# Third and fourth batch: second GroupNorm two batches in front, first convolution's rows in the tail before, convolutions in earlier slots

## The reference

```
x = x + mix(groupnorm(x))       # s = relu(xn.T xn)**2 over the 1024 pixels; y = (W0 x + b0) s
x = x + deform(groupnorm(x))    # offset = conv3x3(conv3x3(x, w1, b1), w2, b2): 72 channels
                                # val = bilinear samples of x at 9 taps x 4 groups, moved by offset
                                # relu(einsum('ogck,bgckhw->bohw', wd, val))
```

## Time and profile before

| | us |
|---|---|
| median of 3 runs (460.49 to 461.5) | 460.77 |
| the profiled execution's own time | 459.05 |
| its span, first to last instruction | 457.0 |
| PE busy, share of the span | 405.2, 89% |
| DVE busy | 339.5, 74% |
| ACT busy | 215.6, 47% |
| POOL busy | 90.0, 20% |
| mean granted TensorE clock (1 is 2.4 GHz) | 0.970 |

### The profile page before, as it was taken

How to read it: one execution, slowest core, us unless ns; L and a number is a source line. 1 busy time by engine, 2 the same in 40 slices (tenths; PEclk the granted TensorE clock), 3 DMA queues, 4 the chain that set the end, 5 groups by cost and what they waited for, 6 DMA issues and landing times.

```text
span 457.0 us, 9689 instructions
## 1 busy us (share of the span) xinstructions
PE 405.2 (89%) x3887; PEld 291.9 (64%) x3887; DVE 339.5 (74%) x586; ACT 215.6 (47%) x392; POOL 90.0 (20%) x99
## 2 busy tenths in 40 slices
PE   6698989979998789799999798989869898979996
PEld 6455557646665565678666575768556566857875
DVE  5995776829999999388854999376979945779901
ACT  3343254345555365441655446331845643257661
POOL 5444470001774100000546100000010000000000
PEclk9899999999999899999999899989979997999999
DMA  7200002250011124332001313442213243303330
GB/s 252 77 0 0 0 2 75 84 141 1 2 47 46 47 67 146 85 90 91 12 13 36 92 54 94 124 126 81 59 47 100 90 122 98 104 23 107 96 105 24
DMA packets 46157, 32.71 MB, mean 72 GB/s; under 512 B 3264, under 2 KB 43488, under 8 KB 46112
## 3 DMA queue, kind: packets, MB, share of 16 engines
q1 hardware_dynamic: 46048, 31.95, 23.5%
q10 hardware_dynamic: 64, 0.13, 0.1%
HBM read 25.24 MB, written 10.37 MB: 78 GB/s over the span
## 4 chain that ended last, share of the span: by engine, by line
PE 46%; DVE 32%; DMA 6%; SPq 5%; issue 4%; ACT 4%; POOL 1%; DVEq 0%; ACTq 0%; POOLq 0%
PE psB L788 10%; PE psB L555 9%; PE psT L739 7%; DVE wpix L1507 7%; PE psV L762 5%; DVE combo L1294 4%; PE psA L646 4%; DMA h_scr<-h_ring 3%; SPq L320 3%; DVE combo_p L1298 2%; DVE tent L1488 2%; PE psA L555 2%; DVE tent L1482 2%; PE psB L813 2%; PE psA L813 2%
## 5 line engine op out<-in xcount | busy, mean ns | idle before, releaser
L1021 ACT ACTIVATE wcell<-psT 128x512 f32<-128x512 f32 (+1 forms) x160 | 83.9, 552 | 70.2 <-PE psT L739 68.9
L1507 DVE TENSOR_TENSOR wpix<-tent 128x512 f32<-128x512 f32 (+1 forms) x160 | 99.7, 675 | 14.4 <-PE psT L739 13.3
L739 PE MATMUL psT<-ident,wpix 128*128 128x128 f32 x576 | 89.1, 288 | 12.4 <-ACT wcell L1021 12.0
L739 PEld LDWEIGHTS psT<-ident,wpix 128*128 128x128 f32 x576 | 68.8, 148 | 37.2 <-issue 29.5
L493 POOL TENSOR_TENSOR sim<-rel 128x512 f32<-128x512 f32 x48 | 61.4, 1299 | 69.0 <-ACT rel L978 69.0
L1045 ACT ACTIVATE val<-psV 128x576 f32<-128x576 f32 x64 | 44.0, 688 | 30.7 <-PE psV L762 30.2
L788 PE MATMUL psB<-val,wd_sb 128*128 128x256 f32 x216 | 51.2, 392 | 0.0
L762 PE MATMUL psV<-wcell,hwin 64*32 64x144 f32 x2048 | 47.2, 294 | 3.9 <-ACT val L1045 3.5
L646 PE MATMUL psA<-sim,scratch 128*128 128x512 f32 x96 | 45.6, 597 | 0.6 <-POOL sim L493 0.6
L788 PEld LDWEIGHTS psB<-val,wd_sb 128*128 128x128 f32 x216 | 40.7, 193 | 8.3 <-issue 2.9
L555 PE MATMUL psB<-g_p 128*128 128x512 f32 x144 | 40.9, 419 | 0.0
(11 more groups left out here) (193 smaller groups left out, 453.6 us busy)
## 6 DMA issues: line engine op xcount, KB each, us to landing
hwin<-h_scr SPq DMA_DIRECT2D x128, 128.0 KB, 2.9
h_scr<-h_ring SPq DMA_DIRECT2D x8, 576.0 KB
h_ring<-sim SPq DMA_DIRECT2D x4, 512.0 KB
x_all<-x SPq DMA_DIRECT2D x1, 1536.0 KB, 10.0
out<-yout SPq DMA_DIRECT2D x12, 128.0 KB, 1.8
off_scr<-sim SPq DMA_DIRECT2D x4, 288.0 KB
combo<-sim SPq DMA_DIRECT2D x32, 32.0 KB
val<-w SPq DMA_DIRECT2D x1, 576.0 KB, 6.1
```

The lines of the kernel that those rows point to most:

```text
L739: last = pe.transpose(bank[:, at:at + P], wpix[:, t % 2, k, 2 * h:2 * h + 2, :].rearrange("p g q -> p (g q)"), ident[:, :])
L1021: act.activation(wcell[:, t % 2, taps[0]:taps[-1] + 1, :, :].rearrange("q k h p -> q (k h p)"), bank[:, 0:len(taps) * G // 2 * P], ACT.Cop ...
L1507: dve.tensor_tensor(w, ty, tx, ALU.mult).then_inc(s["weights_done"], 1)
```

## The change

Batches 2 and 3 get new tables. Their second GroupNorm is done in slots 57 to 60 of the loop two batches before. The rows of their first convolution (four combines, highs and lows) are done in the tail of that loop, in steps -8 to -1 that stand between the tail's instructions. In the loop before theirs the convolutions stand at slots 28 and 41 in place of 36 and 49 for batch 2 (`IN_FRONT`), and spread from slot 4 to 17 and from 26 to 40 for batch 3 (`SPREAD_OUT`); wrapping, turning of offsets and the next weights move up with them. Batch 1's table is unchanged. `lay_image` is issued behind the windows of tile 7 in every loop. The last batch's extremes and the flag move into the fourth loop. Because `combo` is now taken at that time, batch 3's diagonal moves to `sim`.

```diff
+        ROWS_AHEAD = ((-8, -8, -5, -3), (-6, -4, -2, -1), (-8, -7, -4, -2))      # combine, low, high
+        SPREAD_OUT = dict(combine=[ROWS_AHEAD[0], (18, 18, 21, 23)], low=[ROWS_AHEAD[1], (20, 21, 23, 24)],
+                          high=[ROWS_AHEAD[2], (19, 20, 22, 24)], conv=[(4, 7, 8, 13, 16, 17), (26, 29, 31, 34, 35, 40)],
+                          copy=[9, 32], sums=[16, 36], rows=[18, 41], mean=None, dev=None, var=None, norm=None, flat=2,
+                          image=22, wrap=42, shift=None, turn={56: (0, 1), 58: (2, 3)}, extremes=None)
+        AHEAD = dict(mean=57, dev=57, var=59, norm=60)
+        IN_FRONT = dict(in_a_row((29, 35), (30, 36), (28, 41)), mean=None, ..., flat=2, image=27,
+                        wrap=47, shift=None, turn={58: (0, 1), 60: (2, 3)}, extremes=66)
+        LEAD_WEIGHTS, FIRST_WEIGHTS, AHEAD_WEIGHTS, LAST_WEIGHTS, LEAD_EXTREMES = 60, 67, 62, 60, 12
+        LAST_EXTREMES, LAST_FARTHEST, LAST_FLAG = 24, 42, 46
...
 # SyncE
+                    image, shifts = ((5, 7), (4, 6), (5, 6))[min(b, 2)]
-                    if t == IMAGE_TILE + 1 and b + 1 < B:
-                        lay_image(b + 1)
...
                 else:
+                    lay_image(b + 1)
                     for t in range(2):
                         windows(b + 1, t)
...
 # ScalarE, behind the slots
+                rows_ahead(-8, -7)
                 relu_out(b, 0)
+                rows_ahead(-7, -6)
                 take_samples(b, ROWT - 1, 0)
+                rows_ahead(-6, -3)
                 take_samples(b, ROWT - 1, 1)
+                rows_ahead(-3, 0)
                 for m in range(1, 4):
                     relu_out(b, m)
...
 # VectorE, behind the slots
+                rows_ahead(-8)
                 add_out(b, 0)
-                if nxt is not None:
-                    for i in range(len(TAPS)):
-                        weights(nxt, 1, i)
+                for i in range(len(TAPS)):
+                    weights(nxt, 1, i)
+                    rows_ahead(i - 6)
+                rows_ahead(-1)
                 for m in range(1, 4):
                     add_out(b, m)
```

More of the change, by code:

```diff
@@ L881, in batch_steps @@
                                 prepare(prep, what)
-                        if nxt is not None and n == STEADY_IMAGE:
+                        if FIRST_AHEAD <= b + 2 < B:
+                            for col, step in enumerate(("mean", "var")):
+                                if n == AHEAD[step]:
+                                    group_mean(b + 2, col)
+                        if nxt is not None and n == front(nxt)["image"]:
                             turn_image(nxt)
                         if nxt is not None:
-                            conv_front(nxt, n, STEADY, prep)
+                            conv_front(nxt, n, front(nxt), prep)
                 if b == LAST:
@@ L994, in conv_front @@
                     m = 2 * b + which
[L995 to L999, removed]
+                    for v in range(V):
+                        if n == at["high"][which][v]:
+                            act.wait_ge(s["combo_done"], V * m + v + 1)
+                            act.activation(combo_p[:, 0, v], combo[:, v % 2], ACT.Copy).then_inc(s["combo_hi"], 1)
+                    if n == at["copy"][which]:
                         bias, width = ((b1_col, C), (b2_col, NOFF))[which]
@@ L1431, in conv_front @@
                 for which in range(2):
[L1432 to L1436, removed]
+                    for v in range(V):
+                        if n == at["combine"][which][v]:
+                            combine_rows(b, which, v)
+                    for v in range(V):
+                        if n == at["low"][which][v]:
+                            split_rows(b, which, v)
+                    if n == at["sums"][which]:
                         middle_sums(b, which)
-                    if n == at["conv"][which] + 5:
+                    if n == at["rows"][which]:
                         output_rows(b, which)
@@ L1620, in batch_steps @@
                         if nxt is not None:
[L1621 to L1622 removed]
+                            conv_front(nxt, n, front(nxt))
+                        if b == LAST and n == LAST_EXTREMES:
+                            find_extremes(LAST)
+                            find_farthest()
+                        if b == LAST and n == LAST_FLAG:
+                            set_flag()
+                        if FIRST_AHEAD <= b + 2 < B:
+                            if n == AHEAD["dev"]:
+                                spread(b + 2)
+                            if n == AHEAD["norm"]:
+                                normalise_x1(b + 2)
+                        for tile, slots in (W_EVEN if nxt == LAST else W_FRONT if nxt == FIRST_AHEAD else W_AT).items():
                             for i in range(len(TAPS)):
```

96 lines of the change are left out of this document (62 added, 34 removed).

## The result

The changed kernel takes 478.38 us (median of four runs, 476.56 to 480.77), the kernel before 461.05 beside it (460.49 to 461.50): a ratio of 1.0383, 95% interval 1.0345 to 1.0421. It is 17.3 us slower, on the side that was forecast, and 6.4 us above the top of the range. The profiled execution took 480.77 us with a span of 479.0 at a mean granted clock of 0.939 (0.970 before). It is the longest of the four, and the profiled execution of before is shorter than its own median, so the two spans lie 22.0 us apart.

The account below looks back on a forecast made before the run. PE was taken as close to the bound, with its idle time and slow clock in loops 1 and 2 to win. Terms +11.0, +3.0, -11.0 and +1.2 made +4.2 on a median of 460.77: 465.0 us, range 462 to 472.

Parts of the forecast that it names:

- Loop 0's tail: Tail of loop 0: ACT's in-order wait for new rows stops PE; +11.0 us, between +9.3 and +12.8.
- the second stop: Loop 0's tail: PE idle 3 us ahead of piece 2, waiting for the copy of tile 7's second half.
- Loop 1: Loop 1: convolutions and offsets come earlier, but DVE's late chain and clock lengthen it; +3 us, from 0 to +6.
- The chain itself: Loop 1 behind the offsets: DVE's work until 304.0, then 8.2 us to the copy of tile 7's second half.
- the clock's 1.8: Loop 1: three stops of 3 to 4.5 us cost up to 3.5 us of clock; 1.8 taken.
- PE stands about 4.5 us there: Loop 1: PE's wait while the shifted offsets land, where it stood 1.85 us before the change.
- Loop 2: Loop 2: with rows ready and no mixing on DVE, it falls from 84.7 to 73.8 us; -11, from -15 to -6.
- the walk: Loop 2's step-by-step estimate: second convolution's end at 36 us, offsets at 47, loop's end at 71.3 before clock loss.
- Loop 3: Loop 3 and strips: late stores delay DVE's weights, extremes and flag join its list; +1.2 us, 0 to +2.5.
- The flag's own wait is covered by 16 slots.: Loop 3: the flag is set early enough that PE does not wait for it; no cost booked.
- 1 to 2 us in tile 5: Loop 3: PE's wait for weights because DVE starts some 4 us late and has extremes to do.
- much slower: Rival: tail stops keep PE at 1.2 GHz through pieces 2 and 3, every term at its upper end; +15, 476 us; chance 0.12.

Follow-up runs that it names:

- e1: Changed kernel with one edit: in ACT's tail, piece 0 and both halves of tile 7 stand ahead of the rows' highs; 467.73 us, ratio 1.0177.
- e2: Changed kernel with one edit: SP issues a tail's first two stores ahead of the next batch's windows; 475.55 us, ratio 1.0346.
- e3: Changed kernel with one number changed: DVE sets the flag in slot 36 rather than 46, ahead of tile 6's weights; 474.43 us, ratio 1.0315.
- e4: Changed kernel with 40 unread extra transposes on PE ahead of the wait for shifted offsets in loops 1 and 2; 474.01 us, ratio 1.0287.
- e6: e5 with six of piece 0's dconv taps moved ahead of the offsets' turn in loops 1 and 2; 455.41 us, ratio 0.9883.
- e5: Changed kernel with the edits of e1, e2 and e3 together, nothing else; 462.26 us, ratio 1.0034.
- e9: e6 with two of the four row sets moved from the tail into slots 3 to 9 of the next loop; 451.06 us, ratio 0.9785.
- e10: e6 with the strips issued in the tile after the image again instead of last; 465.28 us, ratio 1.0087.

## Why the prediction was right and wrong

**Loop 0's tail: right.** Forecast +11.0 with bounds 9.3 and 12.8; the loop grew by 12.3, and e1 took 11.1 away with ACT's order alone. The steps came within 0.7 us: the first high ends at 211.92 (forecast 211.20), the copy of tile 7's second half at 218.47 (218.00), piece 2 starts at 218.56 (218.0). Only the second stop is 1.13 us where the forecast has 3, because PE did the work ahead of it at half clock (4.1 us instead of 2.0); DVE's third combine sets its end, so this cost nothing more. The rule of the Trainium skill (Perfetto Trace Analysis, section Per-engine timelines) that ACT takes its list in order is borne out: 7.58 us of waiting on ACT are 5.54 on PE.

**Loop 1: right in sign, mis-sized.** The term was "+3, from 0 to +6"; the loop grew by 9.3 in the profiled execution and by 6.4 in e2 and e3. The offsets turned at 75.95 us into the loop where the forecast has 73.8 (290.4 - 216.6): 2.1. From them to the end the forecast has 31.5 (29.7 and 1.8 of clock); measured are 35.7 (304.27 to 339.94) and, in e2 and e3, some 33, so 1.3 to 4.2 more, and these two sums are the whole miss. The chain itself was right: from the first turned offsets to piece 2 the forecast has 21.8 us (13.6 until DVE reaches the tail, and 8.2), and e4, whose clock holds behind the offsets, takes 21.7 (305.76 to 327.47). The mis-sized term is the clock's 1.8. In the changed kernel the way to piece 2 takes 24.9 (304.27 to 329.18) and pieces 2 and 3 take 10.8 instead of 7.85, 6.0 us too much together; in e3 it is 23.3 and 9.5, 3.2 together. There are three stops (4.67, 2.03, 1.77 us), each followed in the changed kernel by work near 1.2 GHz. How long that lasts differs between executions of the same code, which one profile of before could not show. "PE stands about 4.5 us there" was right (4.67), but the taps behind the stop I booked at full clock; e6 shows that two thirds of them need not stand there at all.

**Loop 2: right in sign, mis-sized.** "-11, from -15 to -6": it fell by 6.8. The stop of the earlier trace rows went, as forecast. The offsets are turned 50.7 us into the loop (390.61) where the walk had 47; these 3.7 are nearly all of the miss of 4.2. The second convolution ends at 378.2, 38.3 us into the loop, where the walk had 36: PE stands 2.6 us ahead of it (0.40, 1.18 and 1.03) where the walk had some 2, and works at a granted clock of 0.61 for the 4.4 us behind the last of these stops, about 1.7 us that the walk has at nothing. The other 1.4 lie between there and the offsets (12.4 where the walk had 11.0).

**Loop 3: wrong.** The failed step is the sentence "The flag's own wait is covered by 16 slots." There are four: the flag stands in slot 46 of DVE's list (`LAST_FLAG`), behind tile 6's weights, and PE waits for it in slot 50 of its own, ahead of the third piece's taps (`LAST_AT`). PE waited 3.46 us for it and then ran at half clock. With the flag in slot 36, fourteen slots ahead, there is no wait and loop 3 falls by 4.4 us (e3), though DVE is as late as before. That DVE started 3.8 us late I had seen ("some 4 us") and priced as a wait of "1 to 2 us in tile 5" (1.72 measured). It is the smaller part of the flag's wait: with DVE on time 2.21 us remain (e2). With both mended the loop stands 1.0 above before (e5). New in DVE's list there are the extremes and the flag's small steps; that they make up the 1.0 is not shown.

**The sum.** Terms of +11.0, +3.0, -11.0, +1.2 made +4.2; with the measured 12.3, 9.3, -6.8 and 7.7, and 0.5 less of lead, it is 22.0 in the profiled executions. Of the miss of 17.8, loop 3 holds 6.5, loop 1 6.3 (half of it that execution's clock), loop 2 4.2, loop 0 1.3. The rival "much slower" (476) lies nearest to the time, and its condition, half clock in the tails, is half met: the 36 matmuls of pieces 2 and 3 took 9.92 us in loop 0 and 10.91 in loop 1, between the 7.85 of 2.4 GHz and twice that. And it had loop 3 at 2.5, where 7.7 came, so that its number comes near is in part luck. Its chance of 0.12 was too small because I let each term's upper end stand alone: a late engine makes PE stop, stops of 3.46 to 5.54 us were each followed by half clock, and the terms then rise together.

## What to carry to other kernels

Where work is moved ahead into a tail, put it on each in-order engine behind the copies on which the bounding engine waits: by ACT's order alone the same rows made loop 0 longer by 12.3 us or by 1.2, though a stop of 2.8 us stays at the start of the next loop. Where a transfer is started earlier, move work of the bounding engine with it, to lie beside the landing; without that the stop moves and the clock behind it is paid again. For each flag, however small its step, count the slots between where one list sets it and where the other waits, and look for what the setting engine has ahead of it: four slots behind a tile's weights were too few even with DVE on time. Keep small transfers that an engine waits for away from large ones issued just ahead on the same queue.

## What the runs showed of the hardware

Stops cost clock too, and not evenly. Behind PE's stops of 3.46 to 5.54 us stands work at a granted clock of 0.50 to 0.60 in the changed kernel. Behind one of 1.90 us in e6 the turn of the offsets ran at full speed (0.34 and 0.29 us a pair of matmuls); behind one of 1.87 us at the same place in e9, which the next rows show, it fell to half speed within two pairs:

```profile
294.14 0.34 PE L712 MATMUL psA<-ident,combo 72*128 72x72 f32 x2 [1.87 <-DMA combo<-sim]
...
294.46 0.45 PE L712 MATMUL psA<-ident,combo 72*128 72x72 f32 x2
```

What decides between the two stays open. And nine transfers of 32 KB issued right behind two of 576 KB came 9.6 us after their last issue instead of 1.9, though nothing on SP itself held them (e10, loop 2); with 17 us between the two it was 1.9 again (e10, loop 1).
